# A graph-attention layer with residual and layer norm: the sum of x and the residual by adding transfers, x tiles asked for one unit ahead, a batch's last block normalised between batches, the closing branches marked

## The reference

```
h  = einsum('bnf,hfo->bhno', x, W)
s1 = einsum('bhno,ho->bhn', h, a1);  s2 = einsum('bhno,ho->bhn', h, a2)
e  = leaky_relu(s1[..., :, None] + s2[..., None, :], 0.2)
attn = softmax(where(adj > 0, e, -9e15), axis=-1)
h_prime = einsum('bhnm,bhmo->bhno', attn, h)      # then (B, N, H*O)
out = layernorm(x + h_prime, eps=1e-5)            # over the 512 features
```

## Time and profile before

| | |
|---|---|
| three runs, us | 3199.03, 3201.51, 3208.34 (median 3201.51) |
| profiled execution | 3208.02 us; its span 3206.2 us |
| TensorE, VectorE busy | 86% each |
| ScalarE, GpSimd busy | 70%, 30% |
| mean granted TensorE clock | 0.969 of full speed |
| bytes moved | 359.19 MB, mean 112 GB/s |

### The profile page before, as it was taken

How to read it: one execution, slowest core, us unless ns; L and a number is a source line. 1 busy time by engine, 2 the same in 40 slices (tenths; PEclk the granted TensorE clock), 3 DMA queues, 4 the chain that set the end, 5 groups by cost and what they waited for, 6 DMA issues and landing times.

```text
span 3206.2 us, 157311 instructions
## 1 busy us (share of the span) xinstructions
PE 2753.7 (86%) x68636; PEld 2400.1 (75%) x68636; DVE 2742.4 (86%) x4210; ACT 2247.7 (70%) x3517; POOL 970.0 (30%) x1043
## 2 busy tenths in 40 slices
PE   5898899888898889988998879998799978998887
PEld 2487776878678786788857878587785878758786
DVE  4898888988889888898888989888897988889887
ACT  2488873878648886488855878468773878738885
POOL 2522216222252223422243221532216222162221
PEclk9899999999999999999999999999999999999998
DMA  5335442444414545144442545325442344423443
GB/s 158 83 96 135 123 112 70 112 131 127 130 52 118 134 123 140 38 131 120 118 134 62 133 115 127 104 79 137 122 122 80 97 128 129 109 81 109 132 126 102
DMA packets 262958, 359.19 MB, mean 112 GB/s; under 512 B 159808, under 2 KB 159808, under 8 KB 262240
## 3 DMA queue, kind: packets, MB, share of 16 engines
q1 hardware_dynamic: 262240, 348.80, 40.5%
HBM read 279.97 MB, written 34.14 MB: 98 GB/s over the span
## 4 chain that ended last, share of the span: by engine, by line
PE 35%; DVE 24%; issue 17%; DMA 9%; ACT 7%; SPq 5%; POOL 1%; DVEq 0%; ACTq 0%; POOLq 0%
PE ps L426 12%; DVE step L693 11%; DMA x_in<-in_x 9%; ACT step L504 7%; PE ps L445 5%; PE ps L446 5%; PE ps L467 5%; PE ps L466 5%; DVE m_neg L717 3%; SPq L276 3%; DVE m_pos L708 2%; DVE y L589 2%; DVE total L564 1%; DVE neg_part L561 1%; SPq L269 1%
## 5 line engine op out<-in xcount | busy, mean ns | idle before, releaser
L504 ACT ACTIVATE step<-s_bc,s_steep 128x512 fp8e4<-128x512 f32 x3072 | 1916.9, 714 | 558.9 <-DVE m_pos L708 479.8
L445 PE MATMUL ps<-b_hi,m_pos 128*128 128x65 f16 x16384 | 1095.7, 196 | 22.8 <-issue 22.2
L446 PE MATMUL ps<-b_lo,m_pos 128*128 128x65 f16 x16384 | 1095.0, 195 | 18.7 <-issue 18.0
L467 PE MATMUL ps<-d_lo,m_neg 128*128 128x65 f16 x16384 | 1054.7, 194 | 33.5 <-issue 33.4
L445 PEld LDWEIGHTS ps<-b_hi,m_pos 128*128 128x128 fp8e5 x16384 | 1063.0, 99 | 24.6 <-issue 24.4
L446 PEld LDWEIGHTS ps<-b_lo,m_pos 128*128 128x128 fp8e5 x16384 | 1062.6, 99 | 25.1 <-issue 24.3
L466 PE MATMUL ps<-d_hi,m_neg 128*128 128x65 f16 x16384 | 1054.9, 194 | 27.8 <-issue 27.3
L466 PEld LDWEIGHTS ps<-d_hi,m_neg 128*128 128x128 fp8e5 x16384 | 1028.4, 98 | 62.8 <-issue 61.6
L467 PEld LDWEIGHTS ps<-d_lo,m_neg 128*128 128x128 fp8e5 x16384 | 1023.2, 98 | 19.4 <-issue 17.5
L708 DVE TENSOR_TENSOR m_pos<-step,maskT 128x1024 uint32<-128x1024 uint32 x512 | 642.8, 1294 | 63.1 <-ACT step L504 30.5
L693 DVE TENSOR_SCALAR step<-s_bc,s_neg 128x512 fp8e5<-128x512 f32 x1024 | 601.3, 650 | 6.4 <-DVE s_neg L652 3.2
(11 more groups left out here) (79 smaller groups left out, 1841.8 us busy)
## 6 DMA issues: line engine op xcount, KB each, us to landing
adj_in<-in_adj SPq DMA_DIRECT2D x266, 512.0 KB, 4.4
s_bc<-s_rows SPq DMA_DIRECT2D x258, 256.0 KB, 3.4
x_in<-in_x SPq DMA_DIRECT2D x144, 256.0 KB, 4.4
y<-in_x SPq DMA_DIRECT2D x32, 1024.0 KB, 7.1
out<-y SPq DMA_DIRECT2D x32, 1024.0 KB, 7.1
maskT<-adj_cut SPq DMA_TRANSPOSE x264, 3.7
W_sb<-in_L_gnn_W SPq DMA_DIRECT2D x4, 256.0 KB, 6.6
s_rows<-sT SPq DMA_DIRECT2D x36, 16.0 KB
```

The source lines that it names most:

```text
L445: pe.matmul(acc, mask, b_hi[:, j, h, :], start=False, stop=False)
L446: mm = pe.matmul(acc, mask, b_lo[:, j, h, :], start=False, stop=(j == JC - 1))
L467: mm = pe.matmul(acc, mask, d_lo[:, j, h, :], start=False, stop=(j == JC - 1))
L504: ins = nc.scalar.activation(chunk(step[qd], c, 0, BLK), s1_bc[h % 2][:], ACT.Relu, bias=s2_steep[:, j, h:h + 1], scale=STEEP, saturate=False)
```

## The change

- `x_sum`: after the first batch's tiles, which GpSimd still adds (now `add_first_x`), GpSimd issues a transfer for each tile that adds the tile from memory to `x_sum`, and waits ahead of the next for the one before. `x_in` has then two readers, not three.
- Residual: `att` is gone and there are two `y` buffers. GpSimd's division writes straight into `y[par]`, and `residual` is one transfer, issued by GpSimd, that adds the block of x to it. SP's load of x into `y` is gone.
- x tiles are asked for in the unit before the one that uses them (`LOAD_UNIT`), and VectorE's `max_x` stands behind the masks instead of ahead of them.
- The last block of a batch: its residual is issued ahead of the next batch's chunks, its statistics come after chunks 11 and 12, GpSimd's `deviation` after chunk 12 and the application after chunk 14, and its store in unit 2. The other blocks keep their places.
- TensorE does the transpose of tile 0 ahead of unit 0's products, and waits for the last positive remainder only ahead of the last chunk's product.
- The five batch loops are built with `hint_back_edge=True`.

```diff
+    LOAD_UNIT = [max(v - 1, 0) for v in TILE_UNIT]
...
-        att = sb("att", [P, IT, H * O], F32)
-        y = sb("y", [P, IT, F], F32)
+        y = [sb(f"y{i}", [P, IT, F], F32) for i in range(2)]
...
             def load_x(xi, slot, pair):
+                if type(xi) is int:
+                    sp.wait_ge(x_added, at(x_added, xi - 1))
                 sp.wait_ge(x_turned, at(x_turned, xi - 1))
                 sp.wait_ge(x_maxed, at(x_maxed, xi - 1))
-                sp.wait_ge(x_summed, at(x_summed, xi - 1))
...
-            with sp.Fori(0, B) as b:
+            with nc.Fori(0, B, engines=[sp.engine], hint_back_edge=True) as b:
...
+                        if unit == 2:
+                            with sp.If(b > 0):
+                                store_block(g - 1, 1)
...
+                        for t in range(JC):
+                            if LOAD_UNIT[t] == unit > 0:
+                                load_x(JC * (b + 1) + t, t % 2, ((b + 1) * (JC // 2) + t // 2) % (NBLK * IT // 2))
...
                         if unit == 0:
+                            pe.wait_ge(hi_d_made, b * JC + JC - 3)
+                            turn_x(JC * (b + 1), 0, (b + 1) * (JC // 2))
                             pe.wait_ge(tiny_made, b + 1)
-                            pe.wait_ge(lo_made, at(lo_made, 2 * JC * (b + 1) - 1))
+
+                            pe.wait_ge(lo_made, at(lo_made, 2 * JC * (b + 1) - 2))
...
+                                if unit == 0 and it == 0 and j == JC - 1:
+                                    pe.wait_ge(lo_made, at(lo_made, 2 * JC * (b + 1) - 1))
+                                    pe.sem_inc(waited[pe.engine], 1)
...
+                    for when, work in ((11, ln_first_half), (12, ln_statistics), (14, ln_apply)):
+                        if jc == when:
+                            with dve.If(b > 0):
+                                work(KB * b - 1, 1)
...
-                        if unit in TILE_UNIT:
-                            t = TILE_UNIT.index(unit)
-                            max_x(JC * (b + 1) + t, t % 2, (b + 1) * (JC // 2) + t // 2, t)
                         if unit == UNITS - 1:
...
                             make_masks(u + 1, h + 1, maskT[k % 2], g * (H // 2) + (h + 1) // 2)
+                        if unit in TILE_UNIT:
+                            t = TILE_UNIT.index(unit)
+                            max_x(JC * (b + 1) + t, t % 2, (b + 1) * (JC // 2) + t // 2, t)
...
+            def add_x(xi, t, odd, pair):
+
+                if t > 0:
+                    pool.wait_ge(x_summed, 16 * xi)
+                    pool.sem_inc(waited[pool.engine], 1)
+                G.dma_start(x_sum[:], x_tiles[bass.ds(pair, 1), odd].rearrange("a p f -> (a p) f"),
+                            accum_op=ALU.add).then_inc(x_summed, 16)
...
                 if h == 0:
-                    pool.wait_ge(y_made, at(y_made, 2 * nth_y))
+                    pool.wait_ge(out_stored, at(out_stored, 16 * (g - 1)))
...
+            def residual(g, par):
                 pool.wait_ge(att_made, at(att_made, UNITS // KB * (g + 1)))
-                for half in range(2):
-                    t = slice(half * IT // 2, (half + 1) * IT // 2)
-                    G.tensor_tensor(y[:, t, :], y[:, t, :], att[:, t, :], ALU.add).then_inc(y_made, 1)
+                pool.sem_inc(waited[pool.engine], 1)
+                G.dma_start(y[par][:].rearrange("p (c e) f -> p c (e f)", e=2),
+                            x_blocks[bass.ds((g + NBLK) % NBLK, 1)].rearrange("a p c f -> (a p) c f"),
+                            accum_op=ALU.add).then_inc(y_made, 16)
...
+                with pool.If(b > 0):
+                    residual(KB * b - 1, 1)
                 for jc in range(JC):
```

More of the change, by code:

```diff
@@ L210, in gat_kernel @@
         lo_made = sem("lo_made", free=1)
+        x_added = sem("x_added", free=2)
         x_sum_turned = sem("x_sum_turned")
@@ L342, in _ @@
                             if k:
[L343 to L353, removed]
+                                store_block(g - 1, (k - 1) % 2)
+            store_block(NBLK - 1, 1)
             sp.wait_ge(out_stored, at(out_stored, 16 * NBLK))
@@ L408, in _ @@
             for fc in range(FC):
-                mm = pe.matmul(ps[:, 0, :], ones[:], y[:, fc, :], start=(fc == 0), stop=(fc == FC - 1))
+                mm = pe.matmul(ps[:, 0, :], ones[:], y[0][:, fc, :], start=(fc == 0), stop=(fc == FC - 1))
             mm.then_inc(w_abs_summed, 1)
@@ L415, in _ @@
             turn_scores(0)
-            with pe.Fori(0, B) as b:
+            with nc.Fori(0, B, engines=[pe.engine], hint_back_edge=True) as b:
                 for jc in range(JC):
@@ L449, in _ @@
                             pe.wait_ge(lo_made, at(lo_made, 2 * JC * (b + 1)))
-                        if unit in TILE_UNIT:
+                        if unit and unit in TILE_UNIT:
                             t = TILE_UNIT.index(unit)
@@ L518, in _ @@
             compare(0, 0, 0)
-            with act.Fori(0, B) as b:
+            with nc.Fori(0, B, engines=[act.engine], hint_back_edge=True) as b:
                 for k in range(KB):
@@ L767, in _ @@
             make_masks(0, 0, maskT[0], 0, 0)
-            with dve.Fori(0, B) as b:
+            with nc.Fori(0, B, engines=[dve.engine], hint_back_edge=True) as b:
                 batch_start(b)
@@ L809, in _ @@
                         for when, work in ((1, ln_first_half), (2, ln_statistics), (3, ln_apply)):
-                            if h == when:
-                                if k:
-                                    work(g - 1)
-                                else:
-                                    with dve.If(b > 0):
-                                        work(g - 1)
-            ln_first_half(NBLK - 1)
-            ln_statistics(NBLK - 1)
-            ln_apply(NBLK - 1)
+                            if h == when and k:
+                                work(g - 1, (k - 1) % 2)
+            ln_first_half(NBLK - 1, 1)
+            ln_statistics(NBLK - 1, 1)
+            ln_apply(NBLK - 1, 1)
         @block.gpsimd
@@ L823, in _, with add_first_x @@
             G = nc.gpsimd
-            def add_x(xi, slot, nth):
-                pool.wait_ge(x_summed, at(x_summed, xi))
+            def add_first_x(i, slot, nth):
+                pool.wait_ge(x_added, at(x_added, i))
                 pool.wait_ge(x_loaded[slot], 16 * (nth + 1))
-                G.tensor_tensor(x_sum[:], x_sum[:], x_in[slot][:], ALU.add).then_inc(x_summed, 1)
+                G.tensor_tensor(x_sum[:], x_sum[:], x_in[slot][:], ALU.add).then_inc(x_added, 1)
+            def add_x(xi, t, odd, pair):
[4 more added lines that the diff above has]
+                            accum_op=ALU.add).then_inc(x_summed, 16)
             def clear_x_sum(n):
@@ L872, in _ @@
             G.nop().then_inc(consts_made, 1)
-            G.nop().then_inc(x_summed, start[x_summed])
+            G.nop().then_inc(x_added, start[x_added])
             G.nop().then_inc(att_made, start[att_made])
             G.nop().then_inc(lo_made, start[lo_made])
-            G.nop().then_inc(y_made, start[y_made])
             for i in range(JC):
-                add_x(i, i % 2, i // 2)
+                add_first_x(i, i % 2, i // 2)
             clear_x_sum(0)
             spread_maxima(0)
-            with pool.Fori(0, B) as b:
+            with nc.Fori(0, B, engines=[pool.engine], hint_back_edge=True) as b:
                 pool.wait_ge(bound_step, 3 * b + 3)
@@ L894, in _ @@
                     G.tensor_tensor(d_lo[:, jc, :, 0:O], full_d, d_hi[:, jc, :, 0:O], ALU.subtract).then_inc(lo_made, 1)
+                    if jc == 12:
+                        with pool.If(b > 0):
+                            deviation(KB * b - 1)
                 pool.wait_ge(bound_taken, b + 1)
@@ L901, in _ @@
                             t = TILE_UNIT.index(unit)
[L902 removed]
+                            add_x(JC * b + t, t, t % 2, ((b + 1) * (JC // 2) + t // 2) % (NBLK * IT // 2))
                         if unit == XSUM_UNIT + 1:
                             clear_x_sum(b + 1)
[L905 to L918 removed]
+                        if h == 3 and k:
+                            deviation(g - 1)
+                        if h == 0 and k:
+                            residual(g - 1, (k - 1) % 2)
+                        if h:
+                            divide_unit(g * H + h - 1, h - 1, g, k % 2)
                         if unit == STAT_UNIT:
@@ L921, in _ @@
                         if h == H - 1:
-                            divide_unit(g * H + h, h, g)
-            residual(NBLK - 1)
+                            divide_unit(g * H + h, h, g, k % 2)
+            residual(NBLK - 1, 1)
             deviation(NBLK - 1)
```

64 lines of the change are left out of this document (24 added, 40 removed).

## The result

The changed kernel takes 3154.32 us (median of four runs, 3151.92 to 3157.01), the kernel before 3200.27 on the same chip (3190.6 to 3208.34). The ratio is 0.985, with a 95% interval of 0.9829 to 0.9871: 1.5% faster, 188 us above the forecast of 2966 and outside its range. The profiled span went from 3206.2 to 3150.6 us.

What follows compares the result with a forecast made beforehand. VectorE was taken to set most units' pace, TensorE less than a microsecond behind; gains of 45.7 us a batch, two thirds felt, gave 8 x 30 = 240 us off, +5 at the end, so 2966 us, range 2870 to 3110.

Steps and rivals of the forecast that it cites:

- What it adds: Batch loop: GpSimd issues 16 + 4 transfers a batch; residual lands in 10 us, hidden; DMA engines some 55% busy.
- Residual by a transfer, and x_sum: Units with GpSimd adds: VectorE's compares and masks no longer stretch; 13.2 us a batch for the residual, 9 for x_sum.
- x tiles one unit ahead: Units with an x tile: xmax's wait of 18.2 us a batch on VectorE goes.
- without the first 3100 us: Rival: the x tiles' early load does nothing, giving 3100 us; no chance of its own given.
- Last block between batches: Last block's normalisation moves from units 1 to 3 into chunks 11 to 15: 5.8 us saved, 3.4 late, per batch.
- Marks: Back edges of the batch loops: VectorE idled 4.13 us there; marking the branches gives 2.9 us a batch.
- The tail: End of program: the residual's transfer replaces 3.5 us of waiting for GpSimd by some 8, +5 us.
- The sum and its two thirds: Whole batch: gains sum to 45.7 us, stalls of two engines overlap, so two thirds, 30 us; 240 us over 8 batches.
- The residual lands late: Rival, VectorE's statistics at h = 1: landing beyond 16 us costs VectorE in 24 blocks, 3350 us at 32; slower 0.09.
- The issue on GpSimd stops VectorE: Rival: each of 20 issues a batch costs VectorE 1.3 us, 26 us a batch, 3174 us; chance 0.07.
- The other direction: Port rule: each GpSimd issue can wait for a run of four VectorE compares, ending before the residual is needed.
- TensorE takes over early: Rival, unit part: TensorE or ScalarE soon sets the pace, a third realised; 3095 us, 3040 to 3190; chance 0.13.

Runs made afterwards that it cites:

- by_head_and_pool_sum: Changed kernel without adding transfers: SP loads x into y plainly, GpSimd adds each head's part in place and adds x_sum from x_in; 3081.25 us.
- tiles_early_only: Kernel before with only the x tiles asked for a unit ahead and max_x behind the masks; 3114.32 us.
- no_adding_transfers: Changed kernel without GpSimd's adding transfers in the batch loop, so the residual and the x_sum of later batches are left out; 2961.88 us.

## Why the prediction was wrong

The step that failed is "What it adds". It costed the new transfers by who waits for their landing: "I take 10 us, hidden", and the added load of the DMA engines, "to some 55%", at nothing. The landing was in fact 11.0 us and hidden. But the engines also carry TensorE's instructions, and once TensorE sets the pace a late block is time lost, and clock with it. That term is 3154.32 - 2961.88 = 192 us, and it was in no rival either. Its parts: the residual's transfers 145, x_sum's 47; cut the other way, 112 us for adding in place of plain, 80 us for the rest. Read from TensorE, in the two profiled executions: 130 us idle for issue, 44 in a lower clock, 9 at the end. The estimate of the load itself was near, 0.59 in the unit part against "some 55%".

The other steps:

- **Residual by a transfer, and x_sum: right.** Compares and masks in a unit with a residual are 2.03 and 2.36 us, where the earlier trace rows had 4.15 and 4.28; over the span the compares fell from 601.3 to 492.3 us. by_head_and_pool_sum shows the reverse, the compares longer again with the adds. (The "eight instructions" of that unit are six, four compares and two masks; the sum doesn't use it.)
- **x tiles one unit ahead: right, and near in size.** VectorE's wait for them fell from 162.8 to 25.6 us, TensorE's by 71, and tiles_early_only gained 81 where the sum's share is 8 x 18.2 x 2/3 = 97. The rival "without the first 3100 us" makes it 134, which doesn't follow from that sum; what the full change would lose without the part was not measured.
- **Last block between batches: right in place.** VectorE's order of time after has its statistics behind chunks 11 and 12 and the application behind chunk 14, as listed:

```profile
887.84 1.27 DVE L578 BATCH_NORM_STATS2 ln_stats<-y 128x6 f32<-128x512 f32 x2
...
891.42 1.27 DVE L582 BATCH_NORM_STATS2 ln_stats<-y 128x6 f32<-128x512 f32 x2
...
898.14 2.71 DVE L595 TENSOR_SCALAR y<-y,ln_mv,ln_rstd 128x512 f32<-128x512 f32 x4
...
913.03 0.43 DVE L568 TENSOR_TENSOR neg_part<-ps,r_row 128x260 f32<-128x260 f32 x1 [9.20 <-PE ps L474]
```

  The wait for the first unit is 9.20 us where it was 8.26. What this move is worth was not run by itself.
- **Marks: right.** 22 us against 23; r_row's wait for issue is 4.3 us in all for seven batches, where one had 4.13.
- **The tail: right.** VectorE's `ln_stats` waited for a residual once, 10.6 us, at the end (some 8 forecast).
- **The sum and its two thirds.** 240 us were forecast for the eight batches, and no_adding_transfers, which has no landing to wait for at the end either, gained 235 on its chip (3196.5 to 2961.9). That nearness is in part luck. The sum counts stalls alone, but of the 234 us between the profiled spans 45 are TensorE's busy time (2753.7 to 2708.5, with the mean clock at 0.969 and 0.982), a term that the forecast didn't have; the time without TensorE busy fell by 188, not by 240.
- **The rivals.** "The residual lands late" fell: VectorE waited for no landing but the last. "The issue on GpSimd stops VectorE" fell: an issue takes 1.24 us, as in the earlier trace rows an add of x_sum did, but VectorE's compares beside an issue alone take 477 ns each (139 of them), and 479 with GpSimd idle (395), and VectorE is busy for 2607.2 us with the transfers and 2603.1 without. The other direction, transfers held up by VectorE's compares, didn't show either: the first packet behind an issue for x_sum came after 1.6 us with compares on VectorE (90 times) and after 1.6 with VectorE idle (16 times). "TensorE takes over early" names the engine, and its stretch up to 3190 holds the measured time, but the mechanism is another: TensorE's busy time didn't grow (2753.7 to 2752.1), and its idle time in all fell (452 to 398) while its part for issue grew from 122.3 to 272.2. (Its point of 3095 is 3087 by its own sum, 3208 - 120 + 5 - 6.5.)

Of what the text said would show it, two lines turned out wrong: "TensorE busy for over 91%", and "no wait for x tiles", of which 25.6 us stayed on VectorE and 37.2 on TensorE. The one under "Wrong" that came is "VectorE waiting for TensorE in most units" (139 of 256). s_bc and adj_in land in 4.0 and 4.8 us, not "much later" than 3.4 and 4.4: the data's own transfers hardly showed what held up TensorE.

What stays open is why a block starts late when the engines are held, and how the 38 us between the residual's transfer and a copy that nobody needs divide.

## What to carry to other kernels

A transfer has two prices: who waits for its landing, and what else needs the DMA engines in those microseconds, the bound engine's instruction blocks among them. Look at an engine that streams tens of thousands of instructions (here 68636 matmuls, a block of 256 instructions per 4 to 6 us) for stops with no releaser in the middle of a product, and at the DMA share beside them. When work is moved from an engine to the DMA engines, ask which engine becomes the bound by that, for it is then that the traffic costs; here small adds spread over the heads (3056 us) beat the adding transfer (3154).

## What the runs showed of the hardware

- TensorE's stops in the products come where a block of 256 instructions ends, and 165 of 174 ended 1.2 to 1.7 us behind the landing of a block. After has 174 of 1.4 us mean, up to 4.6; before has 81 of 1.1 us, no_adding_transfers 123 of 1.1.
- An adding transfer of 1 MB issued by GpSimd lands in 11.0 us, a plain one in 8.1 into the engines' memory and 6.8 between two places in device memory; for the same bytes the adding one holds the DMA engines twice as long (12.6 against 6.4%). One of 256 KB: 4.5 and 3.4 us.
- Copies of 33 MB that nobody waits for cost 15 us in the kernel before, where TensorE waits 153.1 us for masks, and 72 us in no_adding_transfers, where it waits 7.2.
- After a stop of 3.2 us TensorE's granted clock was 0.50 for 3.4 us. Over the span the transfers took the mean from 0.982 to 0.967, 44 us of busy time for the same matmuls.
- Issuing a transfer kept GpSimd busy for 0.9 to 1.4 us and didn't lengthen VectorE's compares beside it (477 against 479 ns), unlike an add.
